# A hybrid block on one core: queries, both mixtures of experts and attention in one program of steps, outputs in halves, the gradient's slope by ScalarE

## The reference

```
# 1 test-time training, 16 heads of 8 numbers
q,k,v = split(ln(x) @ qkv_w + qkv_b);  q,k = normed per head
for _ in range(2):                     # TTT_STEPS
    h = swish(k@gate) * (k@val);  loss = mean((h@proj - v)**2)
    theta -= 0.1 * newton_schulz(grad(loss))   # gate, val, proj; 5 iterations
x += (swish(q@gate) * (q@val)) @ proj @ proj_w + proj_b
# 2 mixture of experts: 8 experts (128x128), the best 2 of each token
g = softmax(ln(x)@Wg + bg);  top 2, scaled to sum 1
x += sum over the 2 of g_e * (ln(x)@We[e] + be[e])
# 3 attention, 16 heads of 64, causal by frames of 32 tokens, per batch
x += softmax(mask(q k^T / 8)) v @ w_out + b_out
# 4 the mixture of experts of part 2 once more, same weights
```

## Time and profile before

| | us |
|---|---|
| median of 3 runs (lowest to highest) | 865.53 (864.76 to 865.62) |
| the profiled execution | 865.99 |
| its span | 864.2 |
| PE, DVE, ACT, POOL busy | 771.1, 557.2, 398.9, 351.4 |
| attention, first scores to last weighing | 463.1 to 797.2 |

### The profile page before, as it was taken

How to read it: one execution, slowest core, us unless ns; L and a number is a source line. 1 busy time by engine, 2 the same in 40 slices (tenths; PEclk the granted TensorE clock), 3 DMA queues, 4 the chain that set the end, 5 groups by cost and what they waited for, 6 DMA issues and landing times. The chain is left out here.

```text
span 864.2 us, 16279 instructions
## 1 busy us (share of the span) xinstructions
PE 771.1 (89%) x5510; PEld 613.1 (71%) x5512; DVE 557.2 (64%) x1649; ACT 398.9 (46%) x1118; POOL 351.4 (41%) x540
## 2 busy tenths in 40 slices
PE   3659999897999888897858999999999999999786
PEld 1239999775999876676645777777777777777765
DVE  3945666444657644675796776776677666665468
ACT  4743333233333323322255766565556555565224
POOL 4855454104888501200372444343334333333027
PEclk9969999997999999897898999999999999999778
DMA  3030000000000000000000000000000000000001
GB/s 104 1 134 2 0 0 0 1 1 1 0 0 0 1 1 1 1 0 2 1 0 1 2 2 3 1 2 2 1 2 1 3 2 1 2 1 2 1 1 50
DMA packets 9457, 7.03 MB, mean 8 GB/s; under 512 B 1584, under 2 KB 9008, under 8 KB 9264
## 3 DMA queue, kind: packets, MB, share of 16 engines
q1 hardware_dynamic: 9392, 6.19, 2.3%
HBM read 5.14 MB, written 1.05 MB: 7 GB/s over the span
## 5 line engine op out<-in xcount | busy, mean ns | idle before, releaser
L1324 POOL TENSOR_SCALAR t_p_<-t_p_,t_rinv_ 128x128 f32<-128x128 f32 (+3 forms) x256 | 132.1, 532 | 202.3 <-DVE t_rinv_ L1520 202.3
L1354 ACT ACTIVATE t_p_<-t_p_,t_nmin_ 128x128 f32<-128x128 f32 (+3 forms) x256 | 140.0, 551 | 9.1 <-DVE t_nmin_ L1513 9.1
L1513 DVE CUSTOM_DVE_ANT_0 t_p_<-t_S_,t_mask_ 128x128 f32<-128x128 f32 (+3 forms) x256 | 112.8, 487 | 21.6 <-PE t_S_ L1411 17.3
L1359 ACT ACTIVATE t_pT_<-t_T_ 128x384 f32<-128x384 f32 (+1 forms) x96 | 50.5, 526 | 118.3 <-PE t_T_ L1423 118.3
L1423 PEld LDWEIGHTS t_T_<-ident,t_p_ 128*128 128x128 f32 x640 | 68.2, 141 | 44.9 <-issue 26.0
L1411 PE MATMUL t_S_<-t_k_,t_q_ 64*128 64x256 f32 (+3 forms) x512 | 95.0, 468 | 0.1
L1423 PE MATMUL t_T_<-ident,t_p_ 128*128 128x128 f32 x640 | 90.9, 281 | 0.3 <-ACT t_pT_ L1359 0.3
L1438 PEld LDWEIGHTS t_O_<-t_pT_,t_v_ 128*64 128x64 f32 x1280 | 69.2, 137 | 11.0 <-ACT t_pT_ L1359 10.5
L1438 PE MATMUL t_O_<-t_pT_,t_v_ 128*64 128x128 f32 x1280 | 76.9, 275 | 0.0
L433 POOL TENSOR_TENSOR g_sp<-g_s,g_t 128x512 f32<-128x512 f32 x32 | 40.8, 1276 | 77.9 <-DVE g_t L560 77.9
L1411 PEld LDWEIGHTS t_S_<-t_k_,t_q_ 64*128 64x128 f32 x512 | 41.5, 185 | 26.9 <-DVE t_nmin_ L1513 12.2
(11 more groups left out here) (261 smaller groups left out, 1863.6 us busy)
## 6 DMA issues: line engine op xcount, KB each, us to landing
wqkv<-in_L_attn_b_w_qkv_dram SPq DMA_DIRECT2D x1, 1536.0 KB
x<-in_L_attn_a_x_dram SPq DMA_DIRECT2D x4, 256.0 KB, 3.5
out_dram<-x SPq DMA_DIRECT2D x4, 256.0 KB, 2.3
we<-in_L_ffn_We_dram SPq DMA_DIRECT2D x1, 512.0 KB
wout<-in_L_attn_b_w_out_dram SPq DMA_DIRECT2D x1, 512.0 KB
proj<-n_L_attn_a_ttt_proj_dram SPq DMA_DIRECT2D x1, 256.0 KB, 5.6
gv<-n_L_attn_a_ttt_gate_dram SPq DMA_DIRECT2D x1, 256.0 KB, 5.1
gv<-in_L_attn_a_ttt_val_dram SPq DMA_DIRECT2D x1, 256.0 KB, 5.6
```

Of the source, the lines that this page charges most:

```text
L1324: last = pool.tensor_scalar(pr[:, G.par, h, cols], pr[:, G.par, h, cols], rinv[:, G.par, n:n + 1], 1.0, ALU.mult, ALU.mult)
L1354: act.activation(pr[:, G.par, h, cols], pr[:, G.par, h, cols], ACT.Exp, bias=nmin[:, G.par, n:n + 1], scale=-1.0, accum_out=rsum[:, G.par, ...
L1359: act.activation(pT[:, G.par, 0, G.blocks], psT[:, 0, 0:G.width], ACT.Copy).then_inc(t["eA"], 1)
L1513: dve.tensor_tensor_reduce(pr[:, G.par, h, cols], psS[:, (2 * G.n + h) % 3, at_:at_ + keys], mask[:, SEQ - keys:SEQ], 1.0, -NEG, ALU.add, ...
```

## The change

- **Loops.** `pipeline` writes all turns out; `unroll` and `each_tile` are gone.
- **Gradient.** ACT takes from G the tanh of G/2 (`g_th`) and, right behind it, the derivative of the swish (`g_slope`); there is no sigmoid and no copy of U. DVE makes `g_sw` = (th+1) times G, which is twice the swish, and the factor 0.5 stands in `g_h` and `g_du`. `g_w` = U times slope is now DVE's. POOL keeps only `k_low` and the weights. `g_sw` waits for both of ACT's results, and the next U product waits for `g_w`.
- **Biases** of the experts are 32x512 (four tiles' blocks) in place of 128x2048, with four DMAs of `be` in place of sixteen. The gate, `projT`, `qkT` and `proj_w` tensors live as long as the kernel.
- **One block.** `second_half_phase` replaces the four last phases. Its steps run from -42 to 126. Chunks of the queries stand in steps -40 to -25, attention's groups in 0 to 95 as before. A `Job` is one mixture of experts for one batch: jobs 0 to 3 are the first mixture, 4 to 7 the second. `FRONT` and `EXPERTS` say in which step each begins. Within a front: moments (+0), normalise (+1), turn, high and low (+2), logits (+3), shift and exponential (+4), routing in three parts (+5 to +7), weights turned (+8), biases (+9). An expert tile takes two steps. A front's vectors are 128x4 or 128x32.
- **Experts:** DVE accumulates 4 of 8, ACT scales 4, POOL adds two at once (128x256) and then the rest (128x128).
- **Root:** POOL raises the variance to the power -0.5 (`power`), where ACT took a square root and DVE a reciprocal. In this part ACT loads tables four times, before seven.
- **Outputs in halves:** after four pairs of a batch the first half of its heads is put out, 4 products per token tile, and added to `x`; after the batch the other (`IN_BATCH` is 24 steps). v has three half buffers in place of two whole ones. All of q, k, v, x, outputs, job products and the weighed values share three banks `psP` in turn.

```diff
-                pipeline(act, (2, keep_hT), (0, k_high), (1, sigmoid), (1, keep_u), (2, dT_high))(base)
+                def tanh(t):
+                    act.wait_ge(g["F"], t.done(1, 2) + 4)
+                    act.wait_ge(g["sw"], t.done(0))
+                    act.activation(th[:, t.ring, :], psG[:, :], ACT.Tanh, scale=0.5).then_inc(g["th"], 1)
+                def derive(t):
+                    act.wait_ge(g["w1"], t.done())
+                    act.activation(slope[:, t.ring, :], psG[:, :], ACT.Derivative_silu).then_inc(g["sp"], 1)
+                pipeline(act, (2, keep_hT), (0, k_high), (1, tanh), (1, derive), (2, dT_high))(base)
-                pipeline(dve, (1, swish), (2, error), (1, hidden), (2, dT_low), (1, fall), (2, grad_val), (2, grad_gate))(base)
+                pipeline(dve, (1, swish), (2, error), (1, hidden), (2, dT_low), (1, gate_factor), (2, grad_val), (2, grad_gate))(base)
...
+    class Job:
+        FRONT = (-32, -27, 2, 20, 34, 58, 82, 106)
+        EXPERTS = (-23, -15, 11, 29, 43, 67, 105, 115)
...
+            def output_of(s):
+                b, n = s // IN_BATCH, s % IN_BATCH
+                where = (b - 1, 1, n - 5) if n < 12 else (b, 0, n - 17)
...
+                def power(kind, n, b):
+                    pool.wait_ge(t["var"], norm_of[kind, n] + 1)
+                    rows = slice(b * TPB, b * TPB + TPB)
+                    pool.tensor_tensor(self.rstd[:, rows], self.lnw[:, 3, rows], self.mhalf[:, rows], ALU.pow).then_inc(t["root"], 1)
+                def add_experts(J, n):
+                    i = J.j * TPB + n
+                    pool.wait_ge(m["y"], i + 1)
+                    pool.tensor_tensor(half[:, :, :], y[:, i % 2, 0:2, :], y[:, i % 2, 2:4, :], ALU.add).then_inc(m["z0"], 1)
...
+                for s in STEPS:
...
+                    for J in jobs(s, 0):
+                        power("m", J.j, J.b)
...
+                    for J, n in tiles(s, 2):
+                        close(J, n)
+                    for J, n in tiles(s):
+                        add_experts(J, n)
...
-            k.query_phase()
-        k.moe_phase(0)
-        k.attention_phase()
-        k.moe_phase(1)
+        k.second_half_phase()
```

More of the change, by code:

```diff
@@ L1294, in attention_phase, with next_q, next_k, values @@
-            uses += [("o", (BATCH - 1) * TPB + m) for m in range(TPB)]
+            def next_q(s):
+                pair = s // 3 + 1
+                return pair if s % 3 == 0 and 0 <= pair < self.PAIRS else None
+            def next_k(s):
+                pair = s // 3 + 1
+                return pair if s % 3 == 1 and 0 <= pair < self.PAIRS else None
+            def values(s):
+                b, p = divmod(s // 3, NP)
+                where = (b, 1, p) if p < TPB else (b + 1, 0, p - TPB)
+                return where if s % 3 == 2 and 0 <= where[0] < BATCH else None
@@ L1308, in _ @@
+            tile_of = lambda n: slice(n * P, n * P + P)
+            @block.sync
+            def _(sp):
+                dst = self.out.rearrange("b (t p) d -> p (b t) d", p=P)
+                for j in range(BATCH, NJ):
+                    rows = Job(j).rows
+                    sp.wait_ge(m["x"], TPB * (j + 1))
+                    sp.dma_start(dst[:, rows, :], x[:, rows, :]).then_inc(m["out"], 16)
+                sp.wait_ge(m["out"], 16 * BATCH)
             @block.gpsimd
             def _(pool):
[L1310 removed]
@@ new lines, in _ @@
+                    if next_q(s) is not None:
+                        take_q(next_q(s))
+                    if in_batch(s, 12) is not None:
+                        take_x(in_batch(s, 12))
+                    for J in jobs(s, TURN):
+                        high(J)
+                    for J in jobs(s, TOP):
+                        gates(J)
+                    for J in jobs(s, WEIGHTS):
+                        high_weights(J)
+                    for J, n in tiles(s):
+                        weigh(J, n)
@@ new lines, in _ @@
+                    for J in jobs(s, TURN):
+                        turn_tokens(J)
+                    for J in jobs(s, LOGIT):
+                        logits(J)
+                    for J in jobs(s, WEIGHTS):
+                        turn_weights(J)
+                    for J in jobs(s, BIAS):
+                        biases(J)
+                    for J, n in tiles(s):
+                        experts(J, n, "eh", 512, m["H"])
+                    for J, n in tiles(s, 1):
+                        experts(J, n, "el", 0, m["E"])
@@ new lines, in _ @@
+                    if query(s, NC + 3) is not None:
+                        stats_of_answer(query(s, NC + 3))
+                    for J, n in tiles(s, 3):
+                        if not J.last:
+                            stats_of_tokens(J, n)
+                    if output_of(s - 1):
+                        stats_of_output(*output_of(s - 1))
+                    if in_batch(s, 10) is not None:
+                        moments(in_batch(s, 10))
+                    for J in jobs(s, 0):
+                        moments(J.b)
@@ new lines, in _ @@
+                    for J in jobs(s, TURN):
+                        low(J)
+                    for J in jobs(s, LOGIT):
+                        take_logits(J)
+                    for J in jobs(s, TOP):
+                        shift(J)
+                    for part in range(3):
+                        for J in jobs(s, ROUTE + part):
+                            route(J, part)
+                    for J in jobs(s, WEIGHTS):
+                        low_weights(J)
+                    for J in jobs(s, BIAS):
+                        add_biases(J)
```

955 lines of the change are left out of this document (449 added, 506 removed).

## The result

The changed kernel takes 882.72 us in the median of four runs (881.58 to 884.43), the kernel before 865.57. It is slower by 17.2 us or 1.98% of these two medians. By either the change is slower; whether by more than 2% is not settled. The profiled execution took 881.58 us with a span of 879.6. The page gives for the engines (busy time, share, instructions)

A forecast was written before the change was run, and what follows sets the result against it. TensorE was taken to bound attention and the gradient stage, the second half's other stages being chains. Head 432, attention 379.5, tail 41 and gradient -1 gave 851.5 us of span, plus 1.3: 853, range 836 to 866.

The forecast's parts named there:

- Gradient, -1: Gradient stage: one old stall gained against possible small new stalls each turn, net -1 us (-3 to +4).
- the 1.5 us taken for a new stall: Gradient stage: error ready at 3.1 to 3.2 us, stalling 0 to 0.1 us a turn over 32 turns; 1.5 taken.
- rival of the gradient's chain: Gradient stage: ACT to DVE to `turn_d` costs 0.1 to 0.3 us more a turn, total 857 to 862; chance 0.1.
- Head, 432: First query product to first scores: steps sum to 83.2 us, first scores at 432 against 463.1, 31 saved (23 to 38).
- two extra table loads: Head: two more ACT table loads, 2.6 us inside ACT's free time; 5.3 by the Trainium skill's switch cost.
- Attention, 379.5: Attention: 334.1 kept, plus 3.5 for half outputs, 35.9 for fronts and expert tiles, and 6 of waits.
- the term for PE's waits: Attention: PE waits 6 us (0 to 15) for all jobs as DVE's load rises to 82%.
- Stays: 334.1: Attention: its own existing work keeps its 334.1 us, before products and waits are added.
- Tail, 41: Behind the last weighing: only job 6's tiles, job 7's front and its tiles remain, 41 us (36 to 46) against 67.0.
- DVE becomes the bound in the short steps: Attention's second and third groups: DVE work uncovered, 35 us in place of 6, total 882; chance 0.15.
- Better overlap: Head, tail and attention: tiles at 1.8 us rather than 2.7 and no attention stalls, total 840 or 838; chance 0.2.
- POOL's power: Layer norms: nearest row 0.21 us; rival has 5 us each, costing 42, total 895; chance 0.05.

The follow-up runs named there:

- experiment 3: Kernel before with only the changed kernel's gradient stage and all pipeline loops written out, bias split left at 128x2048; 866.87 us, ratio 1.0002.
- e19: Changed kernel with attention's moments and norm in steps 6 and 9, fronts of jobs 4 to 6 and experts of jobs 4 and 5 later; 864.12 us, 0.9954.
- e7: Changed kernel with jobs 4 and 5 three steps later, and 13 of 16 routing operations left out for jobs 2 to 6; 876.26 us, ratio 1.0096.
- e6: Changed kernel with all jobs but job 3 moved outside attention; 909.67 us in one run.
- e8: Changed kernel with jobs 4 and 5 three steps later and job 6's experts at step 93 in place of 105; 872.93 us, ratio 1.0065.
- e10: As e8, with the low part of the next batch's input one step later on DVE; 878.12 us, ratio 1.0134.
- e15: As e14, with each job's high and low part treated likewise, logits, shift and routing a step later, job 2 a step earlier; 879.37 us, ratio 1.0129.
- e11: As e10, with the low parts of each job's tokens and weights also a step later; 883.46 us, ratio 1.0194.
- e12: As e11, with v's copy on ACT in place of DVE; 879.65 us, ratio 1.0150.
- e9: As e8, with v's copy on ACT in place of DVE; 871.65 us, ratio 1.0051.
- e14: As e9, with jobs 4 and 5 three more steps later and ACT's high part of the next batch's input ahead of the exponentials; 874.96 us, 1.0080.

## Why the prediction was wrong

The forecast was 853 (851.5 of span); measured were 879.6 of span, 28.1 more: 18.6 in attention, 6.7 in the head, 4.7 in the tail, less 1.9 that came in ahead of them.

- **Gradient, -1.** Its chain was right: with G at 242.22 the slope starts 1.47 later, `g_sw` 2.15 (forecast 2.2), the error ends at 3.04 and `turn_d` stands where it stood, at 3.15.

```profile
242.22 0.48 PE L115 MATMUL g_G<-gvh,g_kh 128*128 128x512 f32 x1
...
243.69 0.59 ACT L453 ACTIVATE g_slope<-g_G 128x512 f32<-128x512 f32 x1
...
244.37 0.69 DVE L539 SCALAR_TENSOR_TENSOR g_sw<-g_th,g_G 128x512 f32<-128x512 f32 x1 [1.91 <-ACT g_slope L453]
...
244.98 0.28 DVE L553 TENSOR_TENSOR g_d<-g_PT,qkv 128x128 f32<-128x128 f32 x1
...
245.37 0.14 PEld L502 LDWEIGHTS g_PT<-ident,g_d 128*128 128x128 f32 x1
```

`turn_d` waits once in each of the two steps, 0.6 and 0.4 us, as it did before (0.5 and 0.5), so the 1.5 us taken for a new stall were not there. The queries start 2.9 us earlier. The lead is 1.1 at the first G product of step 1 (198.46 for 199.59) and 3.8 behind the stall of the earlier trace rows (280.17 for 283.94), so that stall is 2.6 of it. The reason given for that one was wrong: in experiment 3 the bias split has its 2048 columns and takes 4.62 us on POOL, and the stall is gone as well, because the operation it stretched, `g_t` with both inputs in SBUF, is no longer there. Experiment 3 shows too that the gain does not reach the end. The rival of the gradient's chain is refuted.

- **Head, 432.** 435.8. Begun 2.9 earlier and 6.7 longer than the sum. PE waits 4.8 us there for job 1's weights and 4.6 for batch 0's norm, and runs at a mean clock of 0.88. The two extra table loads were hidden:

```profile
380.99 1.28 ACT L1133 ACT_TABLE_LOAD   x1
...
382.29 0.23 ACT L1133 ACTIVATE t_mgate_<-t_mlogit_ 128x32 f32<-128x32 f32 x1
```

PE goes on with its products meanwhile. ACT's operation before this load ends at 380.98 and the one behind it starts where the load ends, so the drain of which the Trainium skill speaks ("ScalarE: Activation LUTs", What ACT_TABLE_LOAD costs) has no room on either side, and its 5.3 us for two switches are not seen.

- **Attention, 379.5.** This step failed, and in it the term for PE's waits: 6 us, 15 at most, against 20.1 and 1.7 more for one fall of the clock (0.79 in 576 to 580 and in 580 to 584). The products were right to 2 us: e19's 380.0 less its 4.7 of waits leaves 375.3, where 373.5 had been summed. What I had wrong is which operations matter. I named the routing and spread DVE's work of a front evenly (9.1 us in the text, though its items add up to 8.7); the runs show that the routing costs little (e7: 1.6 us of attention) and that it is the layer norms in steps without a gap that cost: e19, which moves only fronts and attention's moments and norm, brings 18.1 us of attention back and leaves 4.7 of waits. I had also put attention's own layer norm of the next batch at nothing, in the words "Stays: 334.1". But its moments are new in this stage and its norm went from a first group into a third; in e6, where it stands alone, PE waits 9.2 us.
- **Tail, 41.** 45.7, at the edge of its range (and the sum's own items add up to 40.2). Job 6's operations stand in job 7's chain (DVE waits for its sums at 854.38 ahead of the routing, which ends at 860.4 rather than 856.8 by the sum), and the products run at the lower clock (0.21 apart for the logits, 0.73 as the mean clock of the tail). Experiment 7, without job 6 here, takes 37.5:

```profile
842.88 1.97 DVE L1370 TENSOR_SCALAR qkT<-x,mean,rstd 128x128 f32<-128x128 f32 x4
...
848.23 0.35 PE L115 MATMUL t_P_<-wgh,t_mh_ 128*128 128x8 f32 x1
...
854.38 0.35 DVE L1543 SCALAR_TENSOR_TENSOR t_b_<-t_P_,t_mwt_,t_z_ 128x128 f32<-128x128 f32 x1 [0.77 <-POOL t_z_ L1060]
...
860.53 0.37 PE L1299 MATMUL t_P_<-ident,t_mwt_ 128*32 128x128 f32 x1 [5.23 <-DVE t_mwt_ L1517]
```

- **The rivals.** That DVE becomes the bound in the short steps was given 0.15 and 882 us, and 882.7 came. Its mechanism, DVE's minima late in second and third groups, and its sign were right, its content only in part. That the number fits is luck: it had 29 us more than the sum in attention, where 18.6 came, and the rest was made up by head and tail, of which it says nothing. Better overlap did not come, POOL's power took 1.02 us, between the row of 0.21 and the rival's 5, and its wait is part of the norm's chain.
- The sum of gains was thin to begin with: 48.6 us of head, tail and gradient for 41 us of products put into a stage that had no hole. With no wait at all in attention 7.4 us would have been won (48.6 less the 41.2 between 334.1 and 375.3); 22.8 of waits and slower clock (398.1 less 375.3) made of them 15.4 lost.

What stays open, besides the division of e19's gain: why some of e10 to e15 lost what they did. In e11 attention is 9.7 us longer than in e8, of which 3.1 are waits and 5.2 falls of the clock; in e12 7.4 longer than in e9, with 4.0 of waits and 1.7 more of falls. e10's profiled execution (874.2) is 4 us faster than its median, so part of its loss was not in the profile; in it waits fell by 1.9 and falls of the clock cost 3.4. e14 and e15 have no fall of the clock in attention; e15's first scores come 3.5 us later than e9's and its attention is 2.6 longer, and neither was followed up.
